# New tokens' value projection as half units among the attention's batches, with larger pieces for key tails, new keys and context rows

## What is computed

```python
x = x + xattn(layernorm(x), ctx, ctx, wq, wk, wv, wo)   # cross attention, one head of 1024
q, k_new, v_new = xn @ wq.T, xn @ wk.T, xn @ wv.T       # 512 tokens in all
k = concat([ctx, k_new]); v = concat([ctx, v_new])      # 1601 context rows + 64 new ones per batch
out = softmax(q @ k.T / 32) @ v @ wo.T
x = x + attn(layernorm(x), w_qkv, w_out)                # 16 heads, causal, 64 tokens, rotary
x = x + ffn(layernorm(x), Wg, Wu, Wd, Wr)               # 8 experts, routed
```

## Time and profile before

| | us |
|---|---|
| median of 3 runs | 1305.7 |
| lowest, highest of them | 1304.93, 1308.2 |
| the profiled execution | 1310.41 |
| its span | 1308.3 |
| TensorE busy | 1214.6 (93% of the span) |
| VectorE (DVE) busy | 829.7 (63%) |
| ScalarE (ACT) busy | 628.3 (48%) |
| GpSimd (POOL) busy | 97.2 (7%) |

### The profile page before, as it was taken

The page is one execution under the profiler, slowest core; times in us unless marked ns, Lnnn a source line. Parts: engine busy times, 40 slices in busy tenths (PEclk is TensorE's granted clock), DMA queues, the critical chain, the costliest instruction groups (busy, mean ns, idle before and its releaser), DMA issues.

```text
span 1308.3 us, 18916 instructions
## 1 busy us (share of the span) xinstructions
PE 1214.6 (93%) x7634; PEld 1046.4 (80%) x7634; DVE 829.7 (63%) x1013; ACT 628.3 (48%) x562; POOL 97.2 (7%) x82
## 2 busy tenths in 40 slices
PE   4999989888998899999999399999999999999995
PEld 3888766666766688888888398989999999999894
DVE  7332479999999746645546465656556565656464
ACT  4111279888888733113543244444454445454430
POOL 0000100000000000000000011212111111111101
PEclk9999989999998799999999599999999999999998
DMA  7235299999999763421233356676766766676632
GB/s 297 92 129 193 73 360 359 347 388 368 366 356 380 278 267 131 159 97 65 81 123 129 127 184 213 213 213 202 228 212 203 214 218 207 219 209 222 192 128 32
DMA packets 68053, 277.14 MB, mean 212 GB/s; under 512 B 22456, under 2 KB 22600, under 8 KB 45344
## 3 DMA queue, kind: packets, MB, share of 16 engines
q1 hardware_dynamic: 57312, 245.58, 52.3%
q0 software_dynamic: 10688, 30.81, 9.2%
HBM read 258.02 MB, written 18.35 MB: 211 GB/s over the span
## 4 chain that ended last, share of the span: by engine, by line
PE 72%; DVE 13%; DMA 8%; issue 3%; ACT 2%; POOL 0%; SPq 0%; ACTq 0%; DVEq 0%; POOLq 0%
PE ps L1291 22%; PE ps L1292 21%; PE ps L1293 21%; DVE lo L810 10%; DMA out<-y,target 2%; PE ps L1455 2%; DMA raw_more<-new_values 2%; ACT hi L554 1%; PE ps L1387 1%; PE ps L1677 1%; DMA raw<-context 1%; DMA raw<-new_values 1%; DVE scores L888 1%; DMA raw<-keys 1%; PE ps L1406 1%
## 5 line engine op out<-in xcount | busy, mean ns | idle before, releaser
L810 DVE TENSOR_TENSOR lo<-raw,hi 128x2048 fp32r<-128x2048 f32 (+1 forms) x204 | 458.0, 2258 | 173.7 <-ACT hi L554 171.4
L554 ACT ACTIVATE hi<-raw 128x2048 fp32r<-128x2048 f32 (+1 forms) x204 | 383.3, 1888 | 292.8 <-PE ps L1293 270.7
L1291 PE MATMUL ps<-act_hi,hi 128*128 128x240 f32 (+1 forms) x1152 | 333.3, 289 | 9.9 <-DVE act_lo L833 4.8
L1293 PE MATMUL ps<-act_hi,lo 128*128 128x240 f32 (+1 forms) x1152 | 334.2, 290 | 0.0
L1292 PE MATMUL ps<-act_hi,hi 128*128 128x240 f32 x1024 | 283.1, 276 | 0.0
L1291 PEld LDWEIGHTS ps<-act_hi,hi 128*128 128x128 f32 x1152 | 219.0, 190 | 17.7 <-DVE act_lo L833 5.2
L1293 PEld LDWEIGHTS ps<-act_hi,lo 128*128 128x128 f32 x1152 | 219.6, 191 | 5.2
L1292 PEld LDWEIGHTS ps<-act_hi,hi 128*128 128x128 f32 x1024 | 193.8, 189 | 0.3
L1291 PE MATMUL ps<-hi,act_hi 128*128 128x512 f32 x384 | 151.2, 394 | 0.0
L1293 PE MATMUL ps<-hi,act_lo 128*128 128x512 f32 x384 | 149.7, 390 | 0.0
L1292 PE MATMUL ps<-lo,act_hi 128*128 128x512 f32 x384 | 149.5, 389 | 0.0
(11 more groups left out here) (204 smaller groups left out, 1348.0 us busy)
## 6 DMA issues: line engine op xcount, KB each, us to landing
raw<-weights SPq DMA_DIRECT2D x128, 1024.0 KB, 4.9
raw<-keys SPq DMA_DIRECT2D x32, 1024.0 KB, 10.1
raw<-context SPq DMA_DIRECT2D x32, 1024.0 KB, 9.4
raw_more<-keys SPq DMA_DIRECT2D x16, 1024.0 KB, 10.3
raw_more<-context SPq DMA_DIRECT2D x16, 1024.0 KB, 9.7
xq<-x_in SPq DMA_DIRECT2D x4, 512.0 KB, 6.5
new_keys_t<-kvs POOLq DMA_DIRECT2D x8, 256.0 KB, 3.1
new_values<-kvs POOLq DMA_DIRECT2D x8, 256.0 KB, 2.3
```

Of the source, the lines that this page charges most:

```text
L554: act.activation(part(hi, k, kind), part(raw, k, kind), ACT.Copy).then_inc(hi_done, 1)
L810: dve.tensor_tensor(part(lo, k, kind), part(raw, k, kind), part(hi, k, kind), ALU.subtract).then_inc(lo_done, 1)
L1291: pe.matmul(out, a_hi, b_hi, start=first, stop=False)
L1293: return pe.matmul(out, a_lo, b_hi, start=False, stop=last)
```

## The change

The value weights are laid out like the query's and the key's (stationary) and cut into eight *blocks*, each a half unit: 128 new-value features for all 512 tokens, 24 products. The blocks stand in one list of the attention's units, `ATTENTION`, which all engines walk in place of `step`: a block after the third unit of keys of batches 0 to 4 (five blocks) and of values of batches 0 to 2 (three blocks). A block's result is copied to SBUF by ScalarE, transposed by TensorE (`turn_block`, four transposes) and copied into `new_v`, which stays in SBUF: the new values are neither stored nor loaded.

The new tokens' part of the output is then no longer part of the value units. Their softmax weights are turned by a product of their own, scaled by the reciprocal sums, into `new_p` (`turn_new_weights`). For batches 4 to 7 `turn_o` adds `new_v` x `new_p` (16 products instead of 8). For batches 0 to 3, whose new values are not complete when they end, the turned rows are kept in `q` and finished later (`late`), two of them in each of steps 5 and 6, at values 2 and 5.

Moves of data: new keys are stored as `(B, P, C * QL)`, pieces of 256 B, and loaded as 2 KB a partition; the key tail is loaded as 2112 B a partition; the two parts are put side by side by the splits, which take two instructions for such a unit. Context rows are paired, `(p j)` instead of `(j p)`, so that a partition gets 8 KB at once, and the softmax weights' columns are read with a step of two to match. The last value unit is split over 65 partitions x 1024 elements only. The first new-keys load waits for the 8 key stores. The tail's scores go to bank 5, beside the turned weights. `lorow` is gone: ScalarE copies half the scores straight into `S`.

```diff
+def attention_units():
+    blocks = iter(range(C))
+    def stretch(what, b, extra):
+        for u in range(7):
+            yield what, b, u
+            if u == 2 and extra:
+                yield "block", None, next(blocks)
+    units = list(stretch("keys", 0, True))
+    for s in range(B):
+        if s + 1 < B:
+            units += stretch("keys", s + 1, s < 4)
+        units += stretch("values", s, s < 3)
...
-        new_k_d = nc.dram_tensor("new_keys_t", (P, C, TOK), F32).ap()
+        new_k_d = nc.dram_tensor("new_keys_t", (B, P, C * QL), F32).ap()
-        new_v_d = nc.dram_tensor("new_values", (TOK, D), F32).ap()
...
+            def load_keys(k, b, u):
+                whole = raw_of(k)[:, 0:C * (KTAIL + QL)]
+                load(k, tail_d[b].rearrange("p c n -> p (c n)"), dst=whole[:, 0:C * KTAIL])
+                if b == 0:
+                    for j in range(2):
+                        sp.wait_ge(kv_stored[j], 16 * 4)
+                sp.dma_start(whole[:, C * KTAIL:], new_k_d[b]).then_inc(new_landed, 16)
+            def load_values(k, b, u):
+                    load(k, ctx_d[b, 2 * P * u:2 * P * (u + 1), :].rearrange("(p j) d -> p j d", j=2),
+                    load(k, ctx_d[b, KFULL:KV, :], dst=raw_of(k)[0:KREM, 0:D])
+            def load_block(k, f):
+                load(k, w_d[W_V + f // 2, :, (f % 2) * D:(f % 2 + 1) * D], dst=raw_of(k)[:, 0:D])
...
-                pool.dma_start(new_k_d[:, f, :], kvs[:, f % 2, :]).then_inc(kv_stored[f % 2], 16)
-            for n in range(8):
-                pool.dma_start(new_v_d[t * P:(t + 1) * P, g * HALF:(g + 1) * HALF],
+                pool.dma_start(new_k_d[:, :, f * QL:(f + 1) * QL].rearrange("b p n -> p b n"),
+                               kvs[:, f % 2, :].rearrange("p (b n) -> p b n", b=B)).then_inc(kv_stored[f % 2], 16)
...
+                if kind == KEY_LAST:
+                    act.activation(hi_a, raw_a, ACT.Copy)
+                    act.activation(hi_b, raw_b, ACT.Copy).then_inc(hi_done, 1)
...
+            def block_copy(f):
+                act.wait_ge(block_ready, f + 1)
+                if f > 0:
+                    act.wait_ge(block_turned, f)
+                act.activation(block_t[:, :], ps[:, BLOCK_BANK, :], ACT.Copy).then_inc(block_copied, 1)
...
-            projection(U_V, O_V)
...
+                if u == 6 and s > 0:
+                    pe.wait_ge(pt_split, 2 * s)
+                    pe.wait_ge(rinv_ready, s)
...
+            def turn_new_weights(s):
+                pe.matmul(ps[rows, NEW_P_BANK, 0:QL], S[rows, KV:KEYS], scaled_ident[rows, :],
+            def turn_o(s):
+                for c in range(C):
+                    ins = pe.matmul(out, O[:, c * P:(c + 1) * P], twice[:, 0:QL], start=True, stop=(s < LATE))
+                    if s >= LATE:
+                        ins = pe.matmul(out, new_v[rows, s // 2, c * P:(c + 1) * P], new_p[rows, s // 2, :],
+            def late(b):
+                for c in range(C):
+                    pe.matmul(out, ident, q[:, b, c, :], start=True, stop=False)
+                    ins = pe.matmul(out, new_v[rows, b // 2, c * P:(c + 1) * P], new_p[rows, b // 2, :],
+            def value_block(f, k):
+                for c in range(C):
+                    ins = three(ps[:, BLOCK_BANK, :], hi[:, k % RING, at], lo[:, k % RING, at],
+                                act_hi[:, c, :], act_lo[:, c, :], c == 0, c == C - 1)
+            def turn_block(f, s):
+                for t in range(TT):
+                    ins = pe.transpose(ps[:, NEW_V_BANK, t * P:(t + 1) * P], block_t[:, t * P:(t + 1) * P], ident)
...
+            def attention():
+                for n, (what, b, u) in enumerate(ATTENTION):
+                    if what == "block":
+                        value_block(u, k)
+                    elif what == "keys":
+                        s = b - 1
+                        if u == 2 and s > 0:
+                            turn_o(s - 1)
+                        if u == 4 and s >= 0:
+                            turn_weights(s)
+                        score_block(b, u, k)
+                    else:
+                        if u in (1, 6) and turned_blocks < blocks_before(n):
+                            turn_block(turned_blocks, s)
+                        if u == 2:
+                            turn_new_weights(s)
+                        if s in (5, 6) and u in (2, 5):
+                            late(2 * (s - 5) + u // 3)
+                        values(s, u, k)
```

More of the change, by code:

```diff
@@ L30 @@
 EPS = 1e-5
[L33 to L36, removed]
+FULL, KEY_LAST, VALUE_LAST, BLOCK = "full", "key_last", "value_last", "block"
+def attention_units():
[10 more added lines that the diff above has]
+        units += stretch("values", s, s < 3)
+    assert next(blocks, None) is None
+    return units
+ATTENTION = attention_units()
+U_Q, U_K = 0, 4
+U_KEYS0 = 8
+U_WO = U_KEYS0 + len(ATTENTION)
+LATE = 4
 U_QKV = U_WO + 4
@@ L97, in released @@
         unit("out_ready", O_QK + 2 * (k + 1))
[L98 to L105, removed]
+    for what, b, u in ATTENTION:
+        if what == "block":
+            unit("block_ready", u + 1)
+        elif what == "keys":
+            unit(*(("s_ready", 4 * b + (u + 1) // 2 + (u == 6)) if u % 2 or u == 6 else (None, 0)))
+        else:
+            unit(*(("o_ready", b + 1) if u == 6 else (None, 0)))
     by_tile(O_WO)
@@ L520, in perceiver_block, with scores_at @@
         P_BANK = (6, 6, 2, 6)
-        KEY_LAST, VALUE_LAST = "keys", "values"
+        TAIL_AT = (NCH - 1 - 8) * QL
+        BLOCK_BANK, LATE_BANK, NEW_V_BANK, NEW_P_BANK = 3, 3, 4, 5
+        def scores_at(j, rows):
+            return ps[rows, j, 0:HALF] if j < 3 else ps[rows, 5, TAIL_AT:TAIL_AT + KTAIL + QL]
         def rows_of_step(s):
@@ L624, in step @@
[L624 to L651, removed]
-                    if pos == 13:
-                        act.wait_ge(o_ready, s + 1 + 2 * i)
-                        act.wait_ge(rinv_ready, s + 1 + 2 * i)
-                        if s > 0:
-                            act.wait_ge(ot_ready, s + 2 * i)
-                        act.activation(O[:, :], ps[:, 6:8, :].rearrange("p a n -> p (a n)"),
-                                       ACT.Copy, scale=rinv[:, s % 2:s % 2 + 1]).then_inc(o_norm, 1)
-                if not nxt:
-                    split(k + AHEAD)
@@ new lines, in attention @@
+            def attention():
+                for n, (what, b, u) in enumerate(ATTENTION):
+                    split(U_KEYS0 + n + AHEAD)
+                    if what == "keys":
+                        s = b - 1
+                        if u in (1, 3, 5):
+                            score_add(b, u // 2)
+                        if u == 1 and s > LATE:
+                            turned_lo(s - 1)
+                        if u == 4 and s >= 0:
+                            weights_lo(s)
+                        if u == 6:
+                            score_add(b, 3)
+                            if b == 0:
+                                row_max(0)
+                    elif what == "values":
+                        s = b
+                        if u == 0 and s == B - 1:
+                            turned_lo(s - 1)
+                            weights_lo(s)
+                        if u == 1 and s + 1 < B:
+                            row_max(s + 1)
+                        if u == 1 and s + 2 < B:
+                            q_lo(s + 2)
+                        if s in (5, 6) and u in (2, 5):
+                            late(2 * (s - 5) + u // 3)
@@ L1360, in _ @@
             pe.wait_ge(ln_lo, 2 * TT)
-            for k in range(2 * RING):
+            for k in range(U_KEYS0):
                 def bank_free(j):
@@ L1470, in _ @@
+            attention()
+            pe.wait_ge(late_split, LATE)
+            pe.wait_ge(ot_split, B - 2 - LATE)
             pe.wait_ge(s_evac, 4 * B)
```

511 lines of the change are left out of this document (296 added, 215 removed).

## The result

| | before | changed |
|---|---|---|
| median, us | 1305.33 (4 runs) | 1340.97 (4 runs) |
| lowest to highest | 1304.93 to 1308.2 | 1339.89 to 1342.82 |
| ratio, 95% interval | | 1.0268 (1.0241 to 1.0295) |
| profiled execution | 1310.41 | 1341.82 |
| span | 1308.3 | 1340.0 |

The account below looks back on a forecast made before the run. TensorE was taken to bound the projection and DVE, with late landings, the attention steps. Removing the value projection -43.5, attention +22.6, last turn +1.7: -19.2 us, so 1286.5 us in the median; own range 1278 to 1296, wider 1277 to 1305.

Parts of the forecast that it names:

- The last four batches turn their attended rows with 16 products instead of 8: +1.7 each: Turns of attended rows, batches 4 to 7: 1.7 us more each, priced from a turn of 8 taking 1.7.
- four late turns of 16 products, 3.4 each: Finishing the first four batches, two turns each in steps 5 and 6: 6.8 us of TensorE a step, steps 38.5 each.
- the forecast's place for the end of step 7: Attention's end: start 161.7, less 43.5 for the removed projection, plus 323.2 us of attention (300.6 before).
- step 4: Attention step without blocks or late turns: DVE needs 33.6 us, plus part of the late landings, 35 us.
- Two-block steps: Steps 0 to 2 of the attention: TensorE needs 41.1 us, 42.4 each with waits, laid out by hand.
- One-block step: Step 3 of the attention: TensorE and DVE both need 34.8 us, 2 us lost, 37 us.
- the larger of two needs and 2 us: Rule for step 3: equal TensorE and DVE needs of 34.8 us, plus 2 us lost as before, 37.
- The value projection: Eight chunks of 5.44 us of dense TensorE before the attention leave their place: -43.5 us.
- The stores: New keys stored in 256 B runs: 4 us to landing taken, up to 9 free; SP waits some 10 us.
- Larger pieces: Attention transfers without short runs: 13.4 MB a step at about 410 GB/s, 32.6 us, under DVE's 33.6.
- Two signs named for them: No slice under 380 GB/s in steps 3 and 4; fewer than 1,500 packets under 512 B in the attention.
- The rival that bytes set the rate: Larger pieces bring nothing: plain attention steps 36.6 us, step 3 38.0, kernel 1289; chance 0.13.
- The slower rival: Blocks don't overlap in the attention, split buffers full: two-block steps 47.5 us, kernel 1319, chance 0.10; half of it, 1302, 0.12.

Follow-up runs that it names:

- Kernel 5: Changed kernel with the new tokens' softmax weights zero-padded to 128 partitions per batch, so all products of a turn have 128 rows; 1297.74 us, ratio 0.9934.
- experiment 6: Kernel before the change with the larger pieces alone (key tail, new keys, context rows), value projection and new values left as they were; 1294.44 us, ratio 0.9917.
- experiment 10: On the kernel with spread late turns (1294.24 us): one value block a step, two only in step 0, six late batches; 1301.12 us, ratio 0.9966.
- kernels 1 to 10: The kernels of the ten follow-up runs, variants of the changed kernel or of the kernel before; measured from 1284.14 to 1314.67 us.
- kernels 5 and 9: The second is Kernel 5 with one 512-column identity product per late turn and two of the four late turns moved to step 4; 1294.24 us, ratio 0.9906.
- kernel 3: Changed kernel with the second product of each pair in the turns over all 128 rows, not 64 (part of output wrong); 1297.16 us, one run.

## Why the forecast was wrong

**The step that failed** is "The last four batches turn their attended rows with 16 products instead of 8: +1.7 each" and "four late turns of 16 products, 3.4 each". I priced sixteen products from a row of eight of one kind; these alternate between 128 and 64 rows, and a change costs 0.14 us, two for each pair. They took 5.7 to 8.9 us each, and with them the clock fell, for which the forecast had no term in steps 5 and 6. From the forecast's place for the end of step 7 (161.7 - 43.5 + 323.2 = 441.4) to the measured 482.8 there are 41.4 us, and 37.6 of them are in steps 5, 6 and 7 (56.1, 55.0, 29.5 for 38.5, 38.5, 26). With 128 rows throughout a turn took 3.49 us, and those steps 39.6, 39.6 and 26.4.

**The sum without this error** was still too low. Kernel 5 reached the end of step 7 at 449.4, 8.0 us behind the forecast's place: 2.5 by the end of step 0, 1.9 in steps 1 and 2, 1.6 in step 3, 2.1 in steps 5 and 6, 0.4 in step 7, and 0.6 the other way in step 4. Behind the attention it lost another 2.5. So the price of the turns turned the sign, and of the forecast gain of 19 us these smaller terms took more than half.

**What follows from the turns.** In step 5 three turns took 21.4 us (6.97 + 7.69 + 6.72) instead of 10.5, so 10.9 of the 16.5 over kernel 5's step are theirs. The other 5.6 are the clock: behind a turn the products of 512 columns ran 0.43 apart instead of 0.23, and TensorE was busy for 55.7 of 56.0 us. Part of the 10.9 is the clock too: at full clock three such turns would be 3 x 5.71 = 17.1 us. By this estimate the changes of row count cost 6.7 us of step 5 directly and the lower clock that came with them 9.8. In the output projection the last turn took 7.3 us for 3.4.

**Two-block steps:** 43.4 and 43.3 for a forecast of 42.4. The hand-made order held within 1 us in length; its waits one by one were not compared. One-block step: 38.6 for 37; step 4: 34.5 for 35. The value block costs 38.6 - 34.4 = 4.2 us in a step that had 5.8 us of TensorE free (34.4 - 28.6); I had taken the larger of two needs and 2 us, and that is 1.6 too little for step 3.

**The value projection:** gone, -43.5 as forecast; the first score product starts at 115.96 (161.73 before), of which 2.2 us come from an earlier key projection that the change doesn't touch; that part is luck.

**The stores:** 3.3 us to landing in the median for 1024 runs of 256 B (2.4 before), one at 7.6, inside the 9 that cost nothing. Stores were no cause; SP stood 21.3 us for them and not some 10, behind full buffers.

**Larger pieces:** right in sign, too small in size. Alone they bring 11 us (8 to 14 by the interval), where experiment 6 expected six to eight. Two signs named for them did not come in the changed kernel: six-microsecond slices of steps 3 and 4 stood at 246 to 423 GB/s, half of them under 380, and the attention (116 to 483 us) had 1,976 packets under 512 B, not fewer than 1,500. The rival that bytes set the rate would have left a plain step at 36.6; step 4 took 34.5, and in the 40 slices above many are at 410 to 426 GB/s. The Trainium skill, *DMA: Bandwidth & Descriptors*, section *Where 436 GB/s comes from*, puts the limit of the memory side at about 358 GB/s: these rows disagree, as those of before did.

**The slower rival** ended on the right side of no change and by the wrong mechanism: blocks do overlap, for a third of their length. Its picture of the full buffers is there in part, as ScalarE's wait at each block (experiment 10). But a block in a step of its own cost 4.2 of its 6.2 us, and 37.6 of the 41.4 us over the forecast are in steps 5 to 7, where no block stands.

**After the attention** the changed kernel was 11 us later still (31.7 in the span for 20.5 at the end of step 7). 7.5 of them come before the first expert's rows are gathered, 5.6 of these in the last turn; 3.7 in the experts' part, which the change doesn't touch and which took 571.6 us before, 568.6 to 573.5 in kernels 1 to 10 and 575.3 here. Why, no run tells.

**Does any of it pay?** The blocks, repaired, are worth nothing measurable: kernels 5 and 9 are at 1297.7 and 1294.2, the pieces alone at 1294.4. The move takes 43.5 us out and puts about the same in (an estimate from these runs): three steps of 43.4 and one of 38.6 for four of 35.5, 27 us; batch 0's block, 6; the turns' products, 9.

## What to carry to other kernels

Price an instruction from a row in which its neighbours are of its kind: sixteen products that alternate between two row counts cost two thirds more than sixteen alike. Where a contraction of 64 rows stands among those of 128, group it or pad it with zeros to the same rows; padding gave the even steps here (39.6 and 39.6, for 40.3 and 44.7 grouped). And work moved into "free" time of an engine cost most of its length here, where the ring between the engines holds only three units ahead: 4 to 5 us for 6.2, and not the larger of two sums. That the ring is the reason is argued from ScalarE's waits; no run had a longer one.

## What was not expected of the hardware

- Each change between a float32 product of 128 rows and one of 64 rows on TensorE cost 0.13 to 0.14 us, with 1, 7 or 15 changes inside a turn; adding to what the product just before it had written cost nothing (0.22 us a product).
- It is not any change of the row count. The changed kernel's step 7 has one product of 64 rows, and later products of 65 rows, among 512-column ones of 128 rows:

```profile
472.48 0.40 PE L1604 MATMUL ps<-lo,pt 128*128 128x512 f32 x1
472.81 0.33 PE L1527 MATMUL ps<-small,scores 64*64 64x64 f32 x2
473.06 0.50 PE L1604 MATMUL ps<-hi,pt 128*128 128x512 f32 x1
...
480.40 0.40 PE L1604 MATMUL ps<-lo,pt 128*128 128x512 f32 x1
480.64 0.40 PE L1604 MATMUL ps<-hi,pt 65*128 65x512 f32 x1
480.87 0.40 PE L1604 MATMUL ps<-lo,pt 65*128 65x512 f32 x1
```

  The product of 64 rows starts 0.33 us behind its neighbour, where the first of a turn with 128 rows started 0.23 behind (kernel 3, 373.74 to 373.97); those of 65 rows start 0.24 and 0.23 apart, as without a change (these are products of split operands with 512 columns; 65 rows among float32 products of 64 columns stand in no run). The kernel before has such a place too: its turn of the softmax weights starts 0.31 behind the key product (298.51 to 298.82), so a sign of the price stood in its trace.
- The granted clock fell to 0.79 to 0.81 over two steps in which TensorE was busy for 55.7 of 56.0 us and 53.7 of 55.0. The Trainium skill, *TensorE: Matmul & The Clock Gate*, section *HAM oscillation*, tells of a clock that falls at waits between bursts; in step 5 there were no such waits (0.3 us idle in all), but turns of 6 to 8 us of alternating small products. With turns of 3.5 us the clock stayed at 1.00 in the same steps; grouped, with turns of 3.75 to 4.4 us, it was 1.00 and 0.89. What makes it fall inside a turn, no run tells.
